# Stacked one-pass attention scores, earlier release of expert weight buffers, and two buffers instead of four in the third expert layer of a four-layer graph and mixture-of-experts kernel

## The chip, the cores and the metric

The kernel runs on one core of a Trainium2 chip. The metric is device time in microseconds (us) of the whole program; smaller is better. Unmarked times below are microseconds.

Engines are named as the profile names them: PE is TensorE, DVE is VectorE, ACT is ScalarE, POOL is GpSimd, SP is SyncE, which here only issues DMAs. PE has a clock with two levels, 1.2 and 2.4 GHz; "half clock" below means the lower.

## The reference, cut to what matters

1024 tokens (graph nodes) of 256 features pass four layers. Each layer adds a graph attention or graph convolution to x, then a mixture of experts with two experts per token:

```python
x = x + _L0_gnn_ref(_layernorm(x), neigh, edge_emb, adj, ...)
x = x + _L0_ffn_ref(_layernorm(x)[None], ...)[0]
# likewise layers 1, 2 and 3

# layer 0, attention scores (32 hidden features)
neib_att = jnp.tanh(neigh @ Wn1 + bn1) @ Wn2 + bn2
x_att    = jnp.tanh(x @ Wx1 + bx1) @ Wx2 + bx2
e_att    = jnp.tanh(edge_emb[adj] @ We + be)
ws = x_att @ neib_att.T + jnp.einsum('nkh,nh->nk', e_att, x_att)
ws = jax.nn.leaky_relu(ws, 0.01)
ws = jnp.where(adj > 0, ws, jnp.float32(-9000000000000000.0))
ws = jax.nn.softmax(ws, axis=1)

# layer 2, mixture of experts: 8 routed experts, hidden size 1024, and a shared one
shared = gelu(x @ W1s + b1s) @ W2s + b2s
rw = jax.nn.softmax(x @ Wr, axis=-1)
topw, topi = jax.lax.top_k(rw, K)          # K = 2
topw = topw / jnp.sum(topw, axis=-1, keepdims=True)
mask = jnp.sum(jax.nn.one_hot(topi, E) * topw[..., None], axis=-2)
h = gelu(jnp.einsum('bsd,edf->bsef', x, W1p) + b1p)
priv = jnp.einsum('bsef,efd->bsed', h, W2p) + b2p
return shared + jnp.einsum('bsed,bse->bsd', priv, mask)
```

Layer 0 has 16 experts of hidden size 512 with relu, layer 1 has 8 of 512 with gelu, layer 3 has 16 of 512 with a gated silu and no output bias. The adjacency is an integer matrix of zeros and ones, so the edge term takes one of two values per token.

## The kernel before, in words

All engines run programs of their own that meet by semaphores; the order on each engine is the order in which its code is written. Tokens stand in eight tiles of 128 partitions.

**Attention (L209 to L361).** It works in units of 128 query tokens against all 1024 neighbours (eight units in layer 0; more in layer 1, one per tile and head). For unit u: PE computes the scores into the PSUM tile S (`scores`, L516 to L520, layer 0 only; in layer 1 they are a sum of a row and a column and need no matmul). DVE adds the mask and takes the row maximum (`mask`, L241, into g). POOL works out two per-row biases in six tiny operations (L280 to L286). ACT makes the sloped copy (L297, into t2). DVE takes the larger of the two branches (`shift`, L249, into lm). PE transposes lm in eight pieces into the PSUM tile tp (`turn`, L336). ACT takes the exponential from tp (L306, into pT). PE multiplies by the values (`weigh`, L346). DVE divides (L523, L524). In the PE program a step runs turn(u-2), then scores(u+1), which waits until mask(u) has read S, then weigh(u-3). DVE runs mask(u), shift(u-2) and the ending of u-4. There is one S of two PSUM banks, and there are two tp of two banks each.

Ahead of it (the phase p0 of the function that holds L364 to L541) the two score operands g_xa and g_na, 32 partitions of 1024 fp32 values, come out of a matmul (L434) and a DVE operation that adds the bias (L493).

**Experts (L1194 to L1466).** The two choices of each token are sorted by expert into tiles of 128 rows; every expert has whole tiles of its own. Layer 2 has eight tiles for the shared expert ahead of them. The tiles run in rounds of UN = 4: lane b takes every fourth tile, and tile t = 4i + b uses buffer b of the weights w1, w2, b2, of the input rows xs, the output rows ys and the two index columns idx and to. The number of rounds is read at run time. A weight load is issued only when the expert of the tile differs from the one that its buffer holds. A round is never cut, so the tile count is a multiple of four.

For tile t:

- SP (L1262 to L1285) waits for y_ready of tile t-UN, that is for the last use of buffer b, then issues w1, w2 and b2.
- POOL (L1289 to L1315) runs load(t), which gathers 128 rows from DRAM into xs (L1308; a plain copy, L1302, for the shared tiles) once tile t-UN has been turned; then store(t-UN-1), which waits for y_ready of that tile and scatters ys to DRAM (L1293).
- PE runs turn(t) (L1333, transposes xs), rise(t-1) (L1345, first matmul, 32 or 16 pieces), fall(t-2) (L1358, second matmul in three passes of rounded parts).
- ACT runs w2_hi(t) (L1381, rounds w2), the activation of t (L1393; for silu L1386), h_hi(t) (L1397, rounds h).
- DVE runs copy(t) (L1408) and the next index column (L1413), split_w2(t-1) (L1425), split_h(t-1) (L1430), end(t-2) (L1438 and L1440: adds b2, writes ys, signals y_ready).

After the last tile the stored rows are read back and combined (L1125 to L1191), into the SBUF of the w1 buffers.

## Time and profile before

| | |
|---|---|
| median of 3 runs | 1261.8 us (1258.81 to 1266.55) |
| profiled execution | 1265.98 us |
| its span in the trace | 1264.0 us (1.98 us lie outside) |
| mean granted PE clock | 0.863 of full |
| PE busy over the span | 964.2 us (76%) |
| DVE, ACT, POOL busy | 740.7, 511.2, 452.2 us |

The stages that the change touches, as stretches of the trace in us from the span's start:

| stage | stretch | PE busy | PE clock |
|---|---|---|---|
| attention of layer 0 | 49 to 109 | 48.79 of 60 | 0.77 |
| experts of layer 0 | 152 to 246 | 83.98 of 94 | 0.98 |
| experts of layer 1 | 476 to 560 | 74.84 of 84 | 0.97 |
| experts of layer 2 | 697 to 905 | 207.00 of 208 | 0.99 |
| experts of layer 3 | 1092 to 1236 | 142.47 of 144 | 0.98 |

A row of the timeline gives start, duration, engine, line of the kernel, operation, tiles out<-in and shapes; a number before "x" is how many pieces stand in the row, and square brackets give the idle time of the engine just before it and what ended it. A tile name in the trace has its buffer number left out, so e_xs is any of the xs buffers of a layer. "DMA e_w<-w_in" is a weight load, "DMA e_b<-b_in" a load of b2.

### The profile page before, as it was taken

To read this page: it belongs to the slowest core of one execution; us is meant where nothing else is said; L and a number is where in the kernel's file an instruction comes from. 1 tells how busy PE (TensorE), PEld (TensorE's weight loads), DVE (VectorE), ACT (ScalarE), POOL (GpSimd) and SP (SyncE) were. 2 spreads that over 40 slices of the span, in tenths; PEclk is the share of its full clock that TensorE was granted. 3 is DMA by queue.
4 is the path that set the end of the run, shared out by engine and by line. 5 is a ranking of instruction groups with operands and counts; after the bars stand their busy time and mean duration, and the time that the engine had idled before them with its cause. 6 is when DMAs were issued, how large, how long until landed. Compare 5 with 4: busy or idle time off the path is not lost. (4 is left out here: it accounts for less than half of the span.)

```text
span 1264.0 us, 22113 instructions
## 1 busy us (share of the span) xinstructions
PE 964.2 (76%) x7102; PEld 875.1 (69%) x7102; DVE 740.7 (59%) x1712; ACT 511.2 (40%) x941; POOL 452.2 (36%) x572
## 2 busy tenths in 40 slices
PE   5786389808688738955973999999928995499993
PEld 1555288804677738854873899999914884499993
DVE  4435567664688655657434566666553674566664
ACT  2032067600366516642101777777603551243441
POOL 1031246410599514630000255555303440244431
PEclk9677599957799958987995899999958996699997
DMA  6001296520000015743112654653240001544764
GB/s 217 1 1 35 88 316 221 166 85 7 1 1 1 2 56 186 254 158 104 55 30 96 263 199 166 235 196 128 76 129 1 1 1 35 219 155 160 249 238 160
DMA packets 65605, 148.31 MB, mean 117 GB/s; under 512 B 10464, under 2 KB 42496, under 8 KB 59520
## 3 DMA queue, kind: packets, MB, share of 16 engines
q1 hardware_dynamic: 55552, 120.17, 27.7%
q0 software_dynamic: 9984, 27.28, 6.4%
q8 instruction: 37, 0.61, 0.2%
q14 instruction: 32, 0.26, 0.1%
HBM read 203.88 MB, written 18.87 MB: 176 GB/s over the span
## 5 line engine op out<-in xcount | busy, mean ns | idle before, releaser
L1345 PE MATMUL r_pH<-e_xsT,e_w 128*128 128x128 f32 x2624 | 319.4, 280 | 13.8 <-DMA e_w<-w_in 9.7
L1345 PEld LDWEIGHTS r_pH<-e_xsT,e_w 128*128 128x128 f32 x2624 | 308.1, 196 | 20.1 <-issue 12.9
L1293 POOL DMA_INDIRECT y_rows<-e_ys,e_to x104 | 179.3, 1724 | 264.3 <-DVE e_idx L1413 145.3
L1381 ACT ACTIVATE e_w_hi<-e_w 128x1024 fp32r<-128x1024 f32 (+1 forms) x104 | 136.4, 1312 | 128.8 <-DMA e_b<-b_in 95.0
L1425 DVE TENSOR_TENSOR e_w_lo<-e_w,e_w_hi 128x1024 fp32r<-128x1024 f32 (+1 forms) x104 | 161.0, 1548 | 40.7 <-ACT e_w_hi L1381 28.5
L1358 PE MATMUL r_pY<-e_w_hi,e_h_hi 128*128 128x256 f32 x544 | 163.0, 300 | 10.1 <-issue 8.2
L1430 DVE TENSOR_TENSOR e_h_lo<-xnT,e_h_hi 128x512 fp32r<-128x512 f32 (+1 forms) x104 | 89.1, 857 | 124.4 <-ACT e_h_hi L1397 118.3
L1358 PE MATMUL r_pY<-e_w_hi,e_h_lo 128*128 128x256 f32 x544 | 154.5, 284 | 0.0
L1358 PE MATMUL r_pY<-e_w_lo,e_h_hi 128*128 128x256 f32 x544 | 154.5, 284 | 0.0
L346 PE MATMUL g_o<-g_V,g_pT 128*128 128x65 f32 (+2 forms) x896 | 139.2, 310 | 15.3 <-ACT g_pT L306 15.2
L346 PEld LDWEIGHTS g_o<-g_V,g_pT 128*128 128x128 f32 x896 | 124.2, 195 | 31.4 <-issue 21.2
L1308 POOL DMA_INDIRECT e_xs<-xn_rows,e_idx x96 | 102.8, 1070 | 118.1 <-issue 112.2
L1393 ACT ACTIVATE xnT<-r_pH,e_w 128x128 f32<-128x128 f32 x432 | 119.0, 374 | 61.8 <-PE r_pH L1345 58.3
L297 ACT ACTIVATE g_t<-g_g,g_small 128x1024 f32<-128x1024 f32 x56 | 64.4, 1150 | 165.0 <-POOL g_small L286 165.0
L1358 PEld LDWEIGHTS r_pY<-e_w_hi,e_h_hi 128*128 128x128 f32 x544 | 104.7, 192 | 13.2 <-issue 12.7
L1358 PEld LDWEIGHTS r_pY<-e_w_lo,e_h_hi 128*128 128x128 f32 x544 | 105.0, 193 | 0.0
L1358 PEld LDWEIGHTS r_pY<-e_w_hi,e_h_lo 128*128 128x128 f32 x544 | 104.6, 192 | 0.0
L1397 ACT ACTIVATE e_h_hi<-xnT 128x512 fp32r<-128x512 f32 (+1 forms) x104 | 79.3, 762 | 24.1 <-DVE xnT L1420 19.2
L280 POOL TENSOR_TENSOR g_small<-g_small,g_s 128x1 f32<-128x1 f32 x56 | 28.9, 516 | 156.8 <-DVE g_small L241 156.7
L249 DVE SCALAR_TENSOR_TENSOR g_lm<-g_g,g_small,g_t 128x1024 f32<-128x1024 f32 x56 | 71.8, 1282 | 15.5 <-PE g_tp L336 9.5
L121 POOL TENSOR_SCALAR mean_var<-mean_var 128x8 f32<-128x8 f32 x9 | 2.5, 281 | 208.7 <-DVE mean_var L132 192.4
L336 PE MATMUL g_tp<-ident,g_lm 128*128 128x128 f32 x448 | 62.8, 287 | 16.3 <-DVE g_lm L249 15.6
(247 smaller groups left out, 1396.1 us busy)
## 6 DMA issues: line engine op xcount, KB each, us to landing
e_w<-w_in SPq DMA_DIRECT2D x60, 1024.0 KB
e_w<-w_in SPq DMA_DIRECT2D x72, 512.0 KB
e_w<-w_in SPq DMA_DIRECT2D x32, 1028.0 KB
e_w<-w_in SPq DMA_DIRECT2D x44, 514.0 KB
e_b<-b_in SPq DMA_DIRECT2D x76, 128.0 KB
e_w<-y_rows SPq DMA_DIRECT2D x24, 256.0 KB, 5.1
p_adj<-adj_in SPq DMA_DIRECT2D x8, 512.0 KB, 7.0
xn_rows<-xn SPq DMA_DIRECT2D x4, 1024.0 KB, 4.4
```

The lines of the kernel that those rows point to most:

```text
L249: nc.vector.scalar_tensor_tensor(out=lm[u % 2][:, :], in0=g[u % 4][:, :], scalar=b1[:, u:u + 1], in1=t2[u % 4][:, :], op0=ALU.add, op1=ALU ...
L297: nc.scalar.activation(t2[u % 4][:, :], g[u % 4][:, :], ACT.Identity, bias=b2[:, u:u + 1], scale=slope).then_inc(sloped, 1)
L346: ins = nc.tensor.matmul(o[u % 2][:, 0:width], pT[u % 2][:, c, :], values(u, c), start=(c == 0), stop=(c == NT - 1))
L1293: pool.indirect_dma_start(out=y_rows[:, :], in_=ys[b][:, :], in_offset=None, out_offset=bass.IndirectOffsetOnAxis(ap=to[b][:, :], axis=0))\
L1308: pool.indirect_dma_start(out=xs[b][:, :], out_offset=None, in_=xn_rows[:, :], in_offset=bass.IndirectOffsetOnAxis(ap=idx[b][:, :], axis=0))\
L1345: ins = nc.tensor.matmul(pH[b % 2][:, f, :], w1[b][:, at:at + P], xsT[b % 2][:, c, :], start=(c == 0), stop=(c == DC - 1))
L1358: ins = nc.tensor.matmul(pY[m][:, :], h[m][:, f, :], w[m][:, f * D:(f + 1) * D], start=(f == 0 and n == 0), stop=(f == FC - 1 and n == 2))
L1381: nc.scalar.activation(w2_hi[b % 2][:, :], w2[b][:, :], ACT.Copy).then_inc(w2_rounded, 1)
L1393: ins = nc.scalar.activation(hT[b % 2][:, f, :], pH[b % 2][:, f, :], ACT.Relu if kind == "relu" else ACT.Gelu, bias=b1)
L1397: nc.scalar.activation(h_hi[b % 2][:, :, :], hT[b % 2], ACT.Copy).then_inc(h_rounded, 1)
L1425: nc.vector.tensor_tensor(w2_lo[b % 2][:, :], w2[b][:, :], w2_hi[b % 2][:, :].bitcast(F32), ALU.subtract).then_inc(w2_split, 1)
L1430: nc.vector.tensor_tensor(h_lo[b % 2][:, :, :], hT[b % 2], h_hi[b % 2][:, :, :].bitcast(F32), ALU.subtract).then_inc(h_split, 1)
```

## The change

It has three parts.

**A, attention of layer 0.** The operands g_xa and g_na become 96 partitions of the fp32r type: a rounded copy and a remainder, stacked as (high, low, high) against (high, high, low), so that one pass of a 96-row product gives the three partial products. The weights of the matmul ahead are repeated two or three times (three DVE copies), ACT writes the rounded copy over 96 partitions (a new operation of 96x1024, twice), and DVE subtracts over 32 partitions where it added the bias before. Five small bias DMAs are added on SP behind the adjacency loads. S has two buffers and tp one (`deep = 1`). PE starts with scores(0) and scores(1), and then runs scores(u+2) ahead of turn(u-2).

**B, all expert layers.** SP issues w1 once the activation of tile t-UN is done (h_ready; for silu once the first matmul is done, h_summed), w2 once its split is done (w2_split), and b2 two tiles later with a semaphore of its own, b2_loaded. ACT's rounding of w2 no longer waits for b2; DVE's end does. The combine reads into the buffers of w1 and w2.

**C, experts of layer 2.** UN is 2 instead of 4 there: two buffers of everything, rounds of two tiles, four static rounds for the shared tiles. The per-tile tables that depend on UN exist for both values (four more tiny DVE operations at the start).

The core of the diff:

```diff
-UN = 4
+UN_NARROW, UN_WIDE = 4, 2
...
-            tp = [ph.ps(f"tp{n}", [P, NT, P]) for n in range(2)]
+            deep = 1 if scores else 2
+            tp = [ph.ps(f"tp{n}", [P, NT, P]) for n in range(deep)]
...
                     for hf in range(2):
-                        if u >= 2:
-                            pe.wait_ge(exped, 2 * (u - 2) + hf + 1)
+                        if u >= deep:
+                            pe.wait_ge(exped, 2 * (u - deep) + hf + 1)
...
                 if scores:
-                    scores(0).then_inc(scored, 1)
+                    for u in range(2):
+                        scores(u).then_inc(scored, 1)
                 for u in range(units + 3):
+                    if scores and u + 2 < units:
+                        pe.wait_ge(maxed, u + 1)
+                        scores(u + 2).then_inc(scored, 1)
                     if 2 <= u < units + 2:
                         turn(u - 2)
-                    if scores and u + 1 < units:
-                        pe.wait_ge(maxed, u + 1)
-                        scores(u + 1).then_inc(scored, 1)
...
-                xa = ph.sb("xa", [HID, N])
-                na = ph.sb("na", [HID, N])
+                xa = ph.sb("xa", [3 * HID, N], F32R)
+                na = ph.sb("na", [3 * HID, N], F32R)
...
+                        act.wait_ge(again_loaded, 16 * len(again))
+                        for n, (t, ps) in enumerate(((xa, psA), (na, psB))):
+                            act.wait_ge(mm, 3 + n)
+                            nc.scalar.activation(t[:, :].rearrange("p (a b) -> p a b", a=2), ps[0:3 * HID, :, :],
+                                                 ACT.Identity, bias=cols[:, 2 * n + 1:2 * n + 2]).then_inc(rounded, 1)
...
-                        for n, (t, ps) in enumerate(((xa, psA), (na, psB))):
-                            dve.wait_ge(mm, 3 + n)
-                            nc.vector.tensor_scalar(t[:, :].rearrange("p (a b) -> p a b", a=2), ps[0:HID, :, :],
-                                                    cols[:, 2 * n + 1:2 * n + 2], None, ALU.add).then_inc(copied, 1)
+                        for n, (t, lo, ps) in enumerate(((xa, X_LO, psA), (na, N_LO, psB))):
+                            dve.wait_ge(rounded, n + 1)
+                            halves = t[lo, :].rearrange("p (a b) -> p a b", a=2)
+                            nc.vector.scalar_tensor_tensor(out=halves, in0=ps[lo, :, :],
+                                                           scalar=cols[lo, 2 * n + 1:2 * n + 2],
+                                                           in1=halves.bitcast(F32), op0=ALU.add,
+                                                           op1=ALU.subtract).then_inc(copied, 1)
...
+            UN = un = UN_WIDE if shared else UN_NARROW
+            HEAD = max(2, first // UN)
...
                         if not early(i, b, UN):
-                            sp.wait_ge(y_ready, t - UN + 1)
+                            sp.wait_ge(h_summed if kind == "silu" else h_ready, t - UN + 1)
+                            sp.nop(nofuse=True)
                             held = sp.value_load(etab[0:1, bass.ds(t - UN, 1)], min_val=0, max_val=EN - 1)
                             other = {"cond": e != held}
                         sp.dma_start(w1[b][:, :], w1_v[bass.ds(e, 1), :, :].rearrange("a p c -> (a p) c"), **other)\
                             .then_inc(w1_loaded[b], 16)
+                        if not early(i, b, UN):
+                            sp.wait_ge(w2_split, t - UN + 1)
+                            sp.nop(nofuse=True)
                         sp.dma_start(w2[b][:, :], w2_v[bass.ds(e, 1), :, :].rearrange("a p c -> (a p) c"), **other)\
                             .then_inc(w2_loaded[b], 16)
-                        if b2_name:
-                            sp.dma_start(b2[b][:, :], A[b2_name][bass.ds(e, 1), :].to_broadcast([P, D]), **other)\
-                                .then_inc(w2_loaded[b], 16)
+                        if b2_name and not early(i, b, 2):
+                            bias(*before(i, b, 2))
...
-                        act.wait_ge(w2_loaded[b], W2_INC * (i + 1))
+                        act.wait_ge(w2_loaded[b], 16 * (i + 1))
...
                         if b2_name:
+                            dve.wait_ge(b2_loaded[b], 16 * (i + 1))
                             ins = nc.vector.tensor_tensor(ys[b][:, :], pY[b % 2][:, :], b2[b][:, :], ALU.add)
```

**Where it moves instructions: POOL, experts of layer 2.** This is the body of the run-time loop over the rounds of routed tiles, in the kernel before. L1308 is the gather into buffer n of xs, L1293 the store of the rows of a finished tile.

```order
L1308 DMA e2_xs0<-xn_rows,e2_idx0 128x256
L1291 ISA
L1293 DMA y_rows<-e2_ys3,e2_to3 6144x256
L1305 REGISTER_ALU
L1306 REGISTER_ALU
L1308 DMA e2_xs1<-xn_rows,e2_idx1 128x256
L1291 ISA
L1293 DMA y_rows<-e2_ys0,e2_to0 6144x256
```

After, the whole loop body is two tiles long (L1356 is the gather, L1341 the store).

```order
L1356 DMA e2_xs0<-xn_rows,e2_idx0 128x256
L1339 ISA
L1341 DMA y_rows<-e2_ys1,e2_to1 6144x256
L1354 REGISTER_ALU
L1356 DMA e2_xs1<-xn_rows,e2_idx1 128x256
L1339 ISA
L1341 DMA y_rows<-e2_ys0,e2_to0 6144x256
L1278 UNCONDITIONAL_BRANCH
```

The alternation of gather and store is the same. Before, the gather of tile t+1 stands behind the store of tile t-5 (buffer 3, when t has buffer 0); after, it stands behind the store of tile t-3, two tiles younger.

**PE, attention of layer 0, its first units.** Before (L518 scores, L336 transposes of turn, L346 weigh):

```order
L518 MATMUL g0_S<-g0_na,g0_xa 128x512 [waits g0_maxed]
L518 MATMUL g0_S<-g0_na,g0_xa 128x512
L336 MATMUL g0_tp0<-ident,g0_lm0 128x128 [waits g0_shifted]
L336 MATMUL g0_tp0<-ident,g0_lm0 128x128 x7
L518 MATMUL g0_S<-g0_na,g0_xa 128x512 [waits g0_maxed]
L518 MATMUL g0_S<-g0_na,g0_xa 128x512
L336 MATMUL g0_tp1<-ident,g0_lm1 128x128 [waits g0_shifted]
L336 MATMUL g0_tp1<-ident,g0_lm1 128x128 x7
```

After (L543 scores, L338 turn):

```order
L543 MATMUL g0_S0<-g0_na,g0_xa 128x512 [waits g0_maxed]
L543 MATMUL g0_S0<-g0_na,g0_xa 128x512
L338 MATMUL g0_tp0<-ident,g0_lm0 128x128 [waits g0_shifted]
L338 MATMUL g0_tp0<-ident,g0_lm0 128x128 x7
L543 MATMUL g0_S1<-g0_na,g0_xa 128x512 [waits g0_maxed]
L543 MATMUL g0_S1<-g0_na,g0_xa 128x512
L338 MATMUL g0_tp0<-ident,g0_lm1 128x128 [waits g0_exped,g0_shifted]
L338 MATMUL g0_tp0<-ident,g0_lm1 128x128 x3
```

In the piece of before, the scores ahead of turn(0) are those of unit 2 and stand directly behind mask(1); after, they are those of unit 4, and units 0 to 4 have been scored before turn(1). The second turn now also waits for an exponential, since there is one tp.

**SP, experts of layer 0, one step of the loop.** Before:

```order
L1269 ISA [waits e0_y_ready]
L1269 TENSOR_LOAD etab
L1269 ISA x2
L1271 REGISTER_ALU x2
L1271 ISA
L1271 DMA e0_w10<-w1_0_in 128x1028
L1273 ISA
L1273 DMA e0_w20<-w2_0_in 128x1024
L1276 ISA
L1276 DMA e0_b20<-b2_0_in 128x256
```

After:

```order
L1300 ISA [waits e0_h_ready]
L1300 TENSOR_LOAD etab
L1300 ISA x2
L1302 REGISTER_ALU x2
L1302 ISA
L1302 DMA e0_w10<-w1_0_in 128x1028
L1307 ISA [waits e0_w2_split]
L1307 DMA e0_w20<-w2_0_in 128x1024
```

Behind this piece the step goes on with a table read, a wait for y_ready and the DMA of b2 for the tile two before. The load of w1 now waits for the activation, that of w2 for the split, and that of b2 has moved behind them with a wait of its own.

## Rows read from the trace of the kernel before

**Rows 1.** Windows: the expert stages of layers 0, 1, 2, 3.

```profile
core 0: us, PE busy (x) PEld busy (x) DVE busy (x) ACT busy (x) POOL busy (x), PEclk, DMA share, GB/s
...
152.00:246.00 94.00, 83.98 (x674) 79.54 (x675) 60.02 (x135) 61.29 (x136) 51.15 (x42) 0.98 0.76 249
476.00:560.00 84.00, 74.84 (x600) 71.28 (x600) 53.65 (x120) 55.74 (x121) 44.12 (x36) 0.97 0.60 198
697.00:905.00 208.00, 207.00 (x1778) 206.24 (x1777) 129.23 (x179) 156.98 (x311) 103.81 (x57) 0.99 0.52 187
1092.00:1236.00 144.00, 142.47 (x1221) 141.23 (x1222) 87.97 (x185) 59.24 (x80) 61.34 (x49) 0.98 0.63 219
```

**Rows 2.** Timeline, attention of layer 0, one unit at half clock.

```profile
64.06 1.97 PE L336 MATMUL g_tp<-ident,g_lm 128*128 128x128 f32 x8 [2.52 <-DVE g_lm L249]
...
65.96 3.78 PE L518 MATMUL g_S<-g_na,g_xa 32*128 32x512 f32 x4
...
70.92 1.28 DVE L249 SCALAR_TENSOR_TENSOR g_lm<-g_g,g_small,g_t 128x1024 f32<-128x1024 f32 x1
...
72.26 0.93 PEld L336 LDWEIGHTS g_tp<-ident,g_lm 128*128 128x128 f32 x5 [4.10 <-DVE g_lm L249]
```

**Rows 3.** Timeline, attention of layer 0: turns 5, 6 and 7 at full clock.

```profile
92.60 1.09 PE L336 MATMUL g_tp<-ident,g_lm 128*128 128x128 f32 x8 [0.68 <-DVE g_lm L249]
...
98.26 1.09 PE L336 MATMUL g_tp<-ident,g_lm 128*128 128x128 f32 x8 [0.68 <-DVE g_lm L249]
...
103.99 1.04 PE L336 MATMUL g_tp<-ident,g_lm 128*128 128x128 f32 x8
```

**Rows 4.** Timeline, PE, attention of layer 1 (no scores): its turns 0 and 7.

```profile
329.89 1.97 PE L336 MATMUL g_tp<-ident,g_lm 128*128 128x128 f32 x8 [7.83 <-DVE g_lm L249]
...
354.46 1.04 PE L336 MATMUL g_tp<-ident,g_lm 128*128 128x128 f32 x8
```

**Rows 5.** Timeline, PE, layer 2: two successive one-pass matmuls of 256 columns.

```profile
651.22 0.28 PE L724 MATMUL g_pso<-g_high,g_mask 128*128 128x256 f32 x1
651.34 0.28 PE L724 MATMUL g_pso<-g_low,g_mask 128*128 128x256 f32 x1
```

**Rows 6.** Timeline, preparation of layer 0: ACT over 1024 columns, as the added one.

```profile
27.73 1.10 ACT L470 ACTIVATE p_tn<-p_psB,p_cols 32x1024 f32<-32x1024 f32 x1 [2.27 <-PE p_psB L427]
```

**Rows 7.** Waits in the window 152:246 (experts of layer 0): us, times, longest.

```profile
PE r_pH L1345 <- DMA e_w<-w_in: 5.8, 7, 2.0
```

**Rows 8.** Waits in the window 476:560 (experts of layer 1).

```profile
PE r_pH L1345 <- DMA e_w<-w_in: 2.8, 3, 1.6
```

**Rows 9.** Timeline, PE, experts of layer 0: the activation was late.

```profile
200.45 2.05 PE L1345 MATMUL r_pH<-e_xsT,e_w 128*128 128x128 f32 x16 [1.20 <-ACT xnT L1393]
```

**Rows 10.** Timeline, experts of layer 2, steady state: one tile.

```profile
784.88 0.38 PE L1333 MATMUL r_pT<-ident,e_xs 128*128 128x128 f32 x2
...
791.55 0.38 PE L1333 MATMUL r_pT<-ident,e_xs 128*128 128x128 f32 x2
...
793.37 0.42 DVE L1440 TENSOR_TENSOR e_ys<-r_pY,e_b 128x256 f32<-128x256 f32 x1
...
794.10 2.28 DVE L1425 TENSOR_TENSOR e_w_lo<-e_w,e_w_hi 128x2048 fp32r<-128x2048 f32 x1
794.56 2.67 POOL L1293 DMA_INDIRECT y_rows<-e_ys,e_to  x1 [2.72 <-DVE e_idx L1413]
...
797.53 0.97 POOL L1308 DMA_INDIRECT e_xs<-xn_rows,e_idx  x1 [0.30 <-issue]
```

**Rows 11.** Source L1333 in the window 690:905: transposes of layer 2, two a tile.

```profile
L1333 PE MATMUL r_pT<-ident,e_xs x64: 271/273/475, 696.7 to 898.3; 128*128 128x128 f32 x64
```

**Rows 12.** Timeline, POOL: a store in the experts of layer 0.

```profile
183.13 0.99 POOL L1293 DMA_INDIRECT y_rows<-e_ys,e_to  x1 [4.03 <-DVE e_idx L1413]
```

**Rows 13.** DMA view of 744.15:744.50 and 797.48:797.83: gathers, us to landing.

```profile
e_xs<-xn_rows,e_idx POOLq DMA_INDIRECT x1, 6.8
...
e_xs<-xn_rows,e_idx POOLq DMA_INDIRECT x1, 2.8
```

**Rows 14.** Timeline, POOL, experts of layer 2: the first store.

```profile
716.00 3.00 POOL L1293 DMA_INDIRECT y_rows<-e_ys,e_to  x1 [16.99 <-DVE e_ys L1440]
```

126 lines of the change are left out of this document (79 added, 47 removed).

## The prediction

> **What bounds the kernel now.** I read the page first for how full each engine is, then the windows by stage, because the three parts of the change touch stages with different limits, and then the timeline and the waits inside each stage. In the expert stages PE is the bound: in layer 2 it is busy 207.00 of 208 us, in layer 3 142.47 of 144; in layers 0 and 1 it stands idle 10.0 and 9.2 us [rows 1]. So in layers 2 and 3 there is nothing to win except PE work itself, and in layers 0 and 1 at most those gaps. In the attention of layer 0 it is a loop across engines that bounds. At half clock one unit takes 72.26 - 64.06 = 8.20 us, in which the scores alone are 3.78 [rows 2]: scores(u+1) waits for mask(u), mask for scores, and the transposes stand in the same PE queue behind a late shift. At full clock the unit takes 98.26 - 92.60 = 5.66 us, with PE still waiting 0.68 for the shift [rows 3]. The attention of layer 1 runs the same loop without scores; its turns 0 and 7 start at 329.89 and 354.46, so 24.57 us for seven units, a half-clock start included [rows 4].
>
> **Part A, attention of layer 0.** Scores become a one-pass product. Two one-pass matmuls of 256 columns start 0.12 us apart at full clock [rows 5], so 512 columns take 0.24 and a unit's two records 0.48. With two S buffers and the scores two units ahead, the scores leave the cross-engine loop. What is left is the loop of layer 1 with 0.48 us of PE added per unit: 24.57 + 7 x 0.48 = 27.9 us from turn 0 to turn 7. Before it is 103.99 - 64.06 = 39.9 [rows 2, 3]. That gives 12.0. The way to turn 0 held three scores in series with three masks; two of them, at 3.78 each [rows 2], leave it, 7.6 in all, of which I give back 1.0, since the POOL and ACT work of unit 0 then is what the first shift waits for: 6.6. Attention: -18.6. The single tp lets turn(u+1) start only after the exponential of u; weigh(u-1) stands between them on PE and is longer, so I cost it at nothing. If that cover were missing, it would cost one half of an exponential, about 0.6 a unit, 4 in all.
>
> In the preparation ACT gets two operations over 1024 columns like the one of 1.10 us [rows 6]. They take the place of the DVE operation ahead of the subtraction, and the second overlaps the first subtraction, so one of them and its handover stand on the path: +1.3 (bounds 1.1 and 2.5). The repeats of the weights and the five small DMAs stand beside the projections and the adjacency loads; I cost them at nothing, and with the cover gone they would be under 1. Part A: -17.3.
>
> **Part B, release of the weight buffers.** The release moves forward by more than one tile. Waits of PE for weights are 5.8 us in layer 0, in seven places, the longest 2.0 [rows 7], and 2.8 in layer 1, in three places [rows 8]. One more gap of 1.20 in layer 0 is a late activation [rows 9], which stands behind the rounding of w2 on ACT, and that waited for the b2 load that came last. Seven us in layer 0 is thus the most; some loads also compete for bandwidth (249 GB/s on the mean of this stage, [rows 1]) and an earlier issue does not make them shorter. I take 5 of 7 in layer 0, 3 in layer 1 and 1 of the 1.5 idle in layer 3 [rows 1]: -9, with bounds 0 and -14. The added waits on SP (w2_split, y_ready of an older tile) are for things that happened a tile before, so nothing queues behind them for long.
>
> **Part C, two buffers in layer 2.** First the gain. The stage turns 64/2 = 32 tiles [rows 11]. The routing of the reference's inputs gives the eight experts 950, 2, 8, 2, 1015, 50, 8 and 13 rows, hence 8+1+1+1+8+1+1+1 = 22 tiles, with the 8 shared ones 30. In rounds of four they are 32, in rounds of two 30. One tile takes 791.55 - 784.88 = 6.67 us of full PE [rows 10], so two tiles are -13.3.
>
> Then the price. POOL's order is gather(t), store(t-3), gather(t+1). Call T(s) the start of turn(s). The output rows of tile s-2 are complete at 793.37 + 0.42 = 793.79, that is T(s) + 8.91 with T(s) = 784.88; the store starts at T(s) + 9.68 and takes 2.67; the gather behind it starts 0.30 later [rows 10]. With four buffers that gather is for a tile four turns after s and has two tiles of slack. With two buffers it is the gather for tile s+2, so T(s+2) cannot be before T(s) + 9.68 + 2.67 + 0.30 + L = T(s) + 12.65 + L, L the time from the gather's issue to its landing. A gather takes 2.8 with no weights moving and 6.8 in the midst of a weight load [rows 13]. At L = 2.8 two tiles take 15.45 instead of 13.33: PE, full until now, waits 2.12 us in each pair, since turn(s+2) stands ahead of rise(s+1) and fall(s) in its queue.
>
> Weights change at tiles 8 and 9 and at 24 to 29, four pairs. There I take L = 4.3, nearer to the quiet value, because the loads are issued some 6 us before the gather: 16.95, +3.6 a pair. From tiles 4 and 5 on there are twelve pairs: 8 x 2.12 + 4 x 3.6 = 31.4. The loop is entered late as well: the first store runs from 716.00 to 719.00 [rows 14], and gather 4 now stands behind it; with 0.30 and 2.8, T(4) is 722.1, against 784.88 - 10 x 6.67 = 718.2: +3.9. Part C: -13.3 + 31.4 + 3.9 = +22.
>
> Bounds. If every store took the 0.99 us of a store of layer 0 [rows 12], the pair would be 13.77, the twelve pairs +5.3, the entry +1.9, and part C -6. With L = 6.8 in the four loading pairs it is 8 x 2.12 + 4 x 6.1 + 3.9 - 13.3 = +32; in all twelve, which nothing in the quiet tiles speaks for, +64.
>
> Which store applies is told by the trace: it lasts from 794.56 to 797.23, across the DVE operation L1425 (794.10 to 796.38), and a store of layer 0 that stands free takes 0.99 [rows 10, 12]. The extra 1.7 us is about what is left of the DVE operation when the store starts. In the slower loop both still hang on the same event, so I keep 2.67. The Trainium skill, "SBUF — State Buffer", section "Who interferes with whom", bears on this from both sides. A DVE instruction with two SBUF inputs, as L1425 is, contends with a GpSimd instruction that reads SBUF, and the one that comes second is blocked for the whole instruction: by that rule, the trace agrees. The same section infers that a tensor_tensor takes only the read side and leaves descriptor generation alone: by that the store would cost 0.99 and part C be -6; the 2.67 of this trace is against it.
>
> **The sum.** -17.3 - 9 + 22 = -4.3 on the profiled 1265.98 gives 1261.7. The profiled execution is 4.2 above the median of the runs; scaled by 1261.8/1265.98 the forecast is 1257.
>
> **The rivals.**
>
> B: the gather is not late in layer 2. It needs the store to be free of DVE and the gather short, so that the pair stays near 13.3; or weight loads in this loop that move DVE's work away from the store. Then part C is -13 to -6, and the sum -40 to -32: about 1222 to 1230 on the median. For it speaks only that free stores are 0.99 [rows 12]; against it the 2.67 in the steady tile and that even then 13.77 is over 13.33. Chance 0.1.
>
> C, on the slower side: weights and gathers collide more than I take. With two buffers a new expert's 2 MB are asked for only one tile ahead, and the gathers of neighbouring tiles fall into them, also the weight itself can be late for rise. If L is 6.8 in the loading pairs and the loads are late by 2 us in each of the eight loading tiles, part C is +32 + 16 = +48 and the time 1265.98 - 26 + 48 = 1288, or 1284 on the median. It decides from about +39 on. Chance 0.13.
>
> D: part A gives half. PE stays at half clock for most of the attention: the unit then costs twice its PE work, 2 x 3.6 = 7.2, against 8.20 [rows 2], and only the way to turn 0 and the last units gain, about 9 instead of 18.6. The time is 1267. For it speaks that PE has run at half clock until the middle of this stage (8.20 then 5.66); against it that in layer 1 the same loop lost only one or two us to half clock [rows 4] and that PE has fewer gaps after the change. Chance 0.12.
>
> E: part B does nothing, since the loads are bound by bandwidth: 1266. It is a shift inside the forecast's range more than a case of its own. Chance 0.05.
>
> **How the numbers follow.** Forecast 0.6, B 0.1, C 0.13, D 0.12, E 0.05. The likeliest is 1257, its own range 1245 to 1270. For 8 in 10 the range reaches down into the space between it and B and up to the lower part of C: 1238 to 1279. About 1% is what a measurement can tell, so below 1249.2 counts as faster and above 1274.4 as slower. Faster: B, and a quarter of the forecast with part C nearer +14: 0.28. Slower: C, and the tails of D and E: 0.16. Between them 0.56.
>
> **What the profile after would show.** Part A right: turn 7 of layer 0 about 18 us earlier, the time between turns near 3.6 to 4. Part B right: PE's waits for weights in layers 0 and 1 near zero. Part C right: 60 transposes instead of 64; PE's clear waits for "DMA e_xs<-xn_rows,e_idx" at every second turn, of 2 us, where there are none before; turn starts 15.4 us apart over two tiles in the quiet stretch; the gather on POOL right behind a store of 2.7. Part C wrong: turns 6.67 apart, or waits for e_w. The prediction fails by most if the store takes 1 us in layer 2 or the gathers take over 5.

## The result and the profile after

The changed kernel takes 1294.86 us (median of 4 runs, 1290.83 to 1296.89) against 1260.8 of the kernel before on the same chip: a ratio of 1.025, 95% interval 1.0214 to 1.0286. It is slower by 2.5%, on the other side of the forecast of 1257 and outside its range of 1238 to 1279.

The two traces, laid side by side at the same events (us from the span's start; a stage of experts goes from the first transposes of its tiles to the read-back of the stored rows):

| | before | after | difference |
|---|---|---|---|
| scores(0) starts | 49.95 | 51.43 | +1.5 |
| from there to turn 7 of the attention, layer 0 | 54.0 | 29.3 | -24.7 |
| experts of layer 0 | 105.0 | 113.1 | +8.2 |
| experts of layer 1 | 86.5 | 89.9 | +3.4 |
| experts of layer 2 | 224.9 | 269.5 | +44.6 |
| experts of layer 3 | 157.7 | 155.5 | -2.2 |
| span | 1264.0 | 1291.9 | +27.9 |

The attention of layer 0 gave more than forecast, and of the four expert stages two came out with the other sign (layers 0 and 1) and one at twice its size (layer 2). Four turns of the attention after, timeline of PE, which answer to [rows 2, 3]:

```profile
57.57 1.97 PE L338 MATMUL g_tp<-ident,g_lm 128*128 128x128 f32 x8 [0.58 <-DVE g_lm L251]
...
65.23 1.04 PE L338 MATMUL g_tp<-ident,g_lm 128*128 128x128 f32 x8
...
68.37 1.04 PE L338 MATMUL g_tp<-ident,g_lm 128*128 128x128 f32 x8
...
80.74 1.04 PE L338 MATMUL g_tp<-ident,g_lm 128*128 128x128 f32 x8
```

Turn 0 comes 6.1 us after scores(0), against 14.1 before, and a unit with scores at full clock takes 3.14 (65.23 to 68.37) where it took 5.66. PE is at half clock only for the first two units.

The four expert stages after, windows by stage, which answer to [rows 1]:

```profile
core 0: us, PE busy (x) PEld busy (x) DVE busy (x) ACT busy (x) POOL busy (x), PEclk, DMA share, GB/s
129.00:242.00 113.00, 94.11 (x720) 90.28 (x720) 64.56 (x144) 66.27 (x144) 57.23 (x45) 0.92 0.63 212
459.00:549.00 90.00, 76.20 (x600) 73.89 (x600) 53.51 (x120) 55.72 (x121) 48.50 (x37) 0.94 0.58 189
683.00:952.00 269.00, 228.65 (x1740) 223.89 (x1738) 127.56 (x174) 152.60 (x301) 88.96 (x58) 0.89 0.30 104
1122.00:1278.00 156.00, 150.03 (x1288) 149.28 (x1288) 92.58 (x196) 62.08 (x85) 67.24 (x52) 0.98 0.60 207
```

In layer 2 PE runs fewer matmuls than before (30 tiles), yet is busy longer than those need, at a mean granted clock of 0.89 of full where it was 0.99, and 40 us idle. (A timeline row splits a group of matmuls where a window of the view begins, so a rise can stand in one row or in two.) One pair of quiet tiles there, timeline, which answers to [rows 10]:

```profile
790.24 0.43 PE L1381 MATMUL r_pT<-ident,e_xs 128*128 128x128 f32 x2 [2.02 <-DMA e_xs<-xn_rows,e_idx]
790.58 5.44 PE L1393 MATMUL r_pH<-e_xsT,e_w 128*128 128x128 f32 x32
...
791.07 0.97 POOL L1341 DMA_INDIRECT y_rows<-e_ys,e_to  x1 [2.71 <-PE r_pT L1381]
...
792.35 1.98 POOL L1356 DMA_INDIRECT e_xs<-xn_rows,e_idx  x1 [0.30 <-issue]
...
798.72 0.38 PE L1381 MATMUL r_pT<-ident,e_xs 128*128 128x128 f32 x2
798.94 3.74 PE L1393 MATMUL r_pH<-e_xsT,e_w 128*128 128x128 f32 x32
...
800.55 0.42 DVE L1489 TENSOR_TENSOR e_ys<-r_pY,e_b 128x256 f32<-128x256 f32 x1
...
801.74 2.67 POOL L1341 DMA_INDIRECT y_rows<-e_ys,e_to  x1 [7.41 <-DVE e_ys L1489]
...
804.71 0.97 POOL L1356 DMA_INDIRECT e_xs<-xn_rows,e_idx  x1 [0.30 <-issue]
...
807.60 0.43 PE L1381 MATMUL r_pT<-ident,e_xs 128*128 128x128 f32 x2 [2.06 <-DMA e_xs<-xn_rows,e_idx]
```

The chain of the prediction is there link by link: output rows done at 800.97, store from 801.74 for 2.67, gather at 804.71, landed 2.89 later, PE waiting 2.06. What the prediction did not have is in the second row: the rise behind the wait takes 5.44 instead of 3.74. The mean granted clock from 790.58 to 796.00 is 0.69, and from 798.94 to 802.40, in the next rise, 1.00. PE works part of the first at half clock, so the output rows come 10.73 after the turn and not 8.91, and the pair takes 807.60 - 790.24 = 17.36 instead of 15.45.

In layer 0 PE's waits for weights, which were 5.8 us [rows 7], more than doubled (waits view of the window 129:242, changed kernel):

```profile
PE r_pH L1393 <- DMA e_w<-w_in: 12.2, 7, 3.4
```

The same view shows a wait that DVE does not have in the kernel before, where it is ACT that waits for b2. DVE's end of a tile now waits for it, since it is issued two tiles later:

```profile
DVE e_ys L1489 <- DMA e_b<-b_in: 15.2, 13, 3.1
```

And SP has become slow. Its DMA issues in layer 0, timeline of SP, changed kernel (L1302 w1, L1307 w2, L1324 b2):

```profile
166.08 0.34 SPq L1302 DMA_DIRECT2D e_w<-w_in  x1
166.77 0.33 SPq L1307 DMA_DIRECT2D e_w<-w_in  x1
168.67 0.33 SPq L1324 DMA_DIRECT2D e_b<-b_in  x1
170.71 0.33 SPq L1302 DMA_DIRECT2D e_w<-w_in  x1
```

A step of SP takes 4.63 us here, which is also the median of the stage, while a full tile of PE takes 3.43 there. In the kernel before the median step was 3.75. After w2 it goes on for 1.90 us before b2 is issued: two reads of the expert table stand between them.

### The profile page after: what moved, and what is told of

Its sections match the earlier page's. It is cut to its first block and busy times, and to the rows that moved or that the text cites. A ratio compares the mean times of both kernels' runs of the same rounds, so it can differ in the third digit from the quotient of the medians.

```text
span 1291.9 us, 22826 instructions
## 1 busy us (share of the span) xinstructions
PE 959.2 (74%) x6970; PEld 883.3 (68%) x6970; DVE 732.0 (57%) x1707; ACT 504.7 (39%) x923; POOL 439.1 (34%) x568
## 3 DMA queue, kind: packets, MB, share of 16 engines
q1 hardware_dynamic: 53632, 109.01, 24.7%
## 5 line engine op out<-in xcount | busy, mean ns | idle before, releaser
L1393 PE MATMUL r_pH<-e_xsT,e_w 128*128 128x128 f32 x2560 | 338.2, 294 | 21.2 <-DMA e_w<-w_in 17.4
L1393 PEld LDWEIGHTS r_pH<-e_xsT,e_w 128*128 128x128 f32 x2560 | 327.0, 210 | 27.0 <-issue 17.6
L1341 POOL DMA_INDIRECT y_rows<-e_ys,e_to x102 | 163.9, 1607 | 330.6 <-DVE e_ys L1489 195.6
L1429 ACT ACTIVATE e_w_hi<-e_w 128x1024 fp32r<-128x1024 f32 (+1 forms) x102 | 132.4, 1298 | 117.5 <-DMA e_w<-w_in 116.5
L1441 ACT ACTIVATE xnT<-r_pH,e_w 128x128 f32<-128x128 f32 x416 | 115.1, 376 | 128.9 <-PE r_pH L1393 128.9
L1473 DVE TENSOR_TENSOR e_w_lo<-e_w,e_w_hi 128x1024 fp32r<-128x1024 f32 (+1 forms) x102 | 156.0, 1530 | 14.9 <-ACT e_w_hi L1429 14.2
L1406 PE MATMUL r_pY<-e_w_lo,e_h_hi 128*128 128x256 f32 x528 | 150.9, 286 | 0.0
L1406 PE MATMUL r_pY<-e_w_hi,e_h_lo 128*128 128x256 f32 x528 | 150.6, 285 | 0.0
L1356 POOL DMA_INDIRECT e_xs<-xn_rows,e_idx x94 | 105.2, 1119 | 116.7 <-issue 111.9
L1381 PE MATMUL r_pT<-ident,e_xs 128*128 128x128 f32 x204 | 43.1, 298 | 68.3 <-DMA e_xs<-xn_rows,e_idx 55.9
L1381 PEld LDWEIGHTS r_pT<-ident,e_xs 128*128 128x128 f32 x204 | 25.2, 148 | 72.9 <-issue 33.7
```

The lines of the kernel that those rows point to most:

```text
L1341: pool.indirect_dma_start(out=y_rows[:, :], in_=ys[b][:, :], in_offset=None, out_offset=bass.IndirectOffsetOnAxis(ap=to[b][:, :], axis=0))\
L1356: pool.indirect_dma_start(out=xs[b][:, :], out_offset=None, in_=xn_rows[:, :], in_offset=bass.IndirectOffsetOnAxis(ap=idx[b][:, :], axis=0))\
L1381: ins = nc.tensor.transpose(pT[b % 2][:, c, :], xs[b][:, c * P:(c + 1) * P], ident[:, :])
L1393: ins = nc.tensor.matmul(pH[b % 2][:, f, :], w1[b][:, at:at + P], xsT[b % 2][:, c, :], start=(c == 0), stop=(c == DC - 1))
L1406: ins = nc.tensor.matmul(pY[m][:, :], h[m][:, f, :], w[m][:, f * D:(f + 1) * D], start=(f == 0 and n == 0), stop=(f == FC - 1 and n == 2))
L1429: nc.scalar.activation(w2_hi[b % 2][:, :], w2[b][:, :], ACT.Copy).then_inc(w2_rounded, 1)
```

## The experiments

The theory after these readings has three parts. First, in layer 2 the gather stands behind a store that is too young, and the wait that this gives PE lowers its clock, so that each pair pays twice. Second, in layers 0 and 1 SP's own instructions have become the bound, since part B doubled its table reads. Third, part A is sound. The rivals: the new order of the weight loads costs, two buffers are too few as such, or earlier loads collide in the DMA engines.

The runs were taken in four groups. The kernel before ran beside each of them, and its median was 1260.8, 1263.0, 1262.9 and 1264.7 us. A difference between kernels of two groups is uncertain by these few us, and stages are compared within the traces.

**Four buffers in layer 2 again** (e1_four): part C undone.

```diff
-UN_NARROW, UN_WIDE = 4, 2
+UN_NARROW, UN_WIDE = 4, 4
```

> The changed kernel with four buffers and rounds of four in layer 2, parts A and B kept. In the two traces layer 2 (first turn to the read-back of the rows) went from 224.9 to 269.5 us, +44.6. Theory 'part C costs it all': the time falls by 44 to 48 us, to about 1247 to 1251, PE is full again in layer 2. Rival 'the new release order of the weight loads costs in layer 2 too': less than 35 us come back and waits for weights are seen in layer 2.

Measured: 1250.7 us, 44.1 under the changed kernel's 1294.9; layer 2 takes 225.0 us. Against the kernel before the ratio is 0.9881 (0.9847 to 0.9915). The whole loss of layer 2 is part C's, and parts A and B together are worth 12 us, although A alone gives 24 (below). In this trace layer 0 takes 113.4 us and layer 1 93.0, so part B costs there without part C too.

**The store one tile later** (e2_store_later): two buffers stay; POOL stores tile t-4 behind gather t.

```diff
+            LAG = 4 if UN == 2 else UN + 1
...
-                        if not early(i, b, UN + 1):
-                            store(*before(i, b, UN + 1), y_stored[(b - 1) % UN])
+                        if not early(i, b, LAG):
+                            store(*before(i, b, LAG), y_stored[(b - LAG) % UN])
...
-                    store(last - 1, UN - 1, y_stored[UN - 1])
+                    for b in range(2 * UN - LAG, UN):
+                        store(last - 1, b, y_stored[b])
```

> The changed kernel, but in layer 2 POOL stores tile t-4 behind gather t, not tile t-3; two buffers kept. Theory 'the gather stands behind a young store, its wait of 2.0 us at every second turn lowers the clock for the rise behind it': gathers are issued before they are needed, the waits of 2.0 us for e_xs and the rises of 5.4 us go, quiet tiles are 6.7 us apart, layer 2 gives back 44.6 and the two tiles, in all 45 to 58 us: 1234 to 1247. Rival 'two buffers are too few for anything: weights or output rows are late': at most half of that comes back, and waits for e_w or for the stored rows take the place of those for e_xs. Second rival: only the pairs in which weights are loaded stay long, then about 15 us less come back.

Measured: 1239.7 us, 55.2 under the changed kernel; layer 2 takes 215.9 us, 53.6 less than after and 9.0 less than before. The turns of its quiet stretch, timeline of PE, and the store and gather beside them, timeline of POOL:

```profile
792.32 0.38 PE L1383 MATMUL r_pT<-ident,e_xs 128*128 128x128 f32 x2
798.99 0.38 PE L1383 MATMUL r_pT<-ident,e_xs 128*128 128x128 f32 x2
805.66 0.38 PE L1383 MATMUL r_pT<-ident,e_xs 128*128 128x128 f32 x2
```

```profile
788.66 2.67 POOL L1342 DMA_INDIRECT y_rows<-e_ys,e_to  x1 [2.72 <-DVE e_ys L1491]
791.64 0.97 POOL L1357 DMA_INDIRECT e_xs<-xn_rows,e_idx  x1 [0.30 <-issue]
```

Turns are 6.67 apart, without a wait. The store still takes 2.67 and still stands ahead of a gather; only it is one tile older. So two buffers are enough for the weights and the rows in the quiet stretch, and what cost 54 us is the place of one instruction in POOL's order. (At the last tiles, which load new weights, two rises do wait for them, 1.71 and 1.16 us.)

**PE kept busy through the wait** (e4_filler): 14 transposes of the identity ahead of the turn of every even tile from tile 4 on.

```diff
                         if not early(i, b, 2):
                             pe.wait_ge(xsT_ready, t - 1)
+                        if UN == 2 and b == 0 and not early(i, b, 3):
+                            for _ in range(14):
+                                nc.tensor.transpose(pT[b][:, 0, :], ident[:, :], ident[:, :])
                         pe.wait_ge(xs_loaded[b], 16 * (i + 1))
```

> The changed kernel with 14 extra transposes of the identity on PE ahead of the waiting turn of each even tile from 4 on in layer 2, about 1.8 us of PE work in what is otherwise a wait of 2.0 us. Their result is overwritten. Theory 'the wait lowers the clock and the rise behind it pays 1.7 us': the clock stays up, rises take 3.74 instead of 5.4, quiet pairs take about 15.5 instead of 17.3, and the kernel gets 15 to 23 us faster although PE does more. Rival 'the rise is long for another reason': rises stay at 5.4 and the time stays or rises by up to 3 us.

Measured: 1279.5 us, 15.4 under the changed kernel; layer 2 takes 252.8 us, 16.7 less, and its mean granted clock is 0.97. Timeline of PE over one pair:

```profile
783.77 1.69 PE L1381 MATMUL r_pT<-ident 128*128 128x128 f32 x14
...
785.84 0.44 PE L1384 MATMUL r_pT<-ident,e_xs 128*128 128x128 f32 x2 [0.37 <-DMA e_xs<-xn_rows,e_idx]
...
786.16 3.81 PE L1396 MATMUL r_pH<-e_xsT,e_w 128*128 128x128 f32 x32
...
801.48 0.44 PE L1384 MATMUL r_pT<-ident,e_xs 128*128 128x128 f32 x2 [0.46 <-DMA e_xs<-xn_rows,e_idx]
```

PE does more and the kernel is faster: the rise is back at 3.81, and the pair takes 801.48 - 785.84 = 15.64, close to the 15.45 of the prediction. The long rise was the clock, and the idle stretch of PE ahead of it was its cause. The clock's share of part C is thus about 17 us.

**SP without its second pair of table reads** (e3_lean_sp): b2 of tile t is issued in the step of t.

```diff
-                        if b2_name and not early(i, b, 2):
-                            bias(*before(i, b, 2))
+                        if b2_name:
+                            if not early(i, b, UN):
+                                sp.wait_ge(y_ready, t - UN + 1)
+                                sp.nop(nofuse=True)
+                            sp.dma_start(b2[b][:, :], A[b2_name][bass.ds(e, 1), :].to_broadcast([P, D]), **other)\
+                                .then_inc(b2_loaded[b], 16)
```

> The changed kernel, but SP issues b2 of tile t in the step of tile t with the registers it has, so that two reads of the expert table a step go; w1 and w2 are still released early. In the trace of the changed kernel SP's steps in layer 0 are 4.1 to 5.0 us apart, a full PE tile takes 3.43. Theory 'SP's own instructions bound layers 0 and 1': steps come down to PE's pace, waits of PE for weights in layer 0 (13 us) and layer 1 (7 us) fall below those of the kernel before (5.8 and 2.8), total 10 to 20 us faster than the changed kernel. Rival 'earlier loads collide with gathers and each other, bandwidth is the bound': no change, within 4 us.

Measured: 1274.1 us, 20.7 under the changed kernel, with ten executions from 1264.2 to 1280.4. The profiled one is among the shortest, 1264.7 us, so its stages add up to more than the 20.7; why the executions differ by 16 us is open. In its trace layer 0 takes 96.0 us (113.1 in the changed kernel, 105.0 before) and layer 1 81.2 (89.9 and 86.5). SP's timeline in layer 0, and PE's wait for weights there (window 120:240):

```profile
172.01 0.34 SPq L1302 DMA_DIRECT2D e_w<-w_in  x1
172.70 0.34 SPq L1307 DMA_DIRECT2D e_w<-w_in  x1
173.37 0.33 SPq L1313 DMA_DIRECT2D e_b<-b_in  x1
175.51 0.33 SPq L1302 DMA_DIRECT2D e_w<-w_in  x1
```

```profile
PE r_pH L1383 <- DMA e_w<-w_in: 0.2, 1, 0.2
```

A step is 3.50 us instead of 4.63, b2 follows w2 after 0.67 instead of 1.90, and 12.2 us of waits shrink to 0.2. w1 and w2 are released as early as in the changed kernel, so collisions of the early loads are not the cause. The edit does two things at once, though: it takes out two reads, and it issues b2 two tiles earlier, which also ends DVE's 15.2 us of waits for b2. The next run tells how much the reads do alone. Two reads cost 1.90 - 0.67 = 1.23 us, 0.6 each. The Trainium skill, "DMA: Bandwidth & Descriptors", section "Latency and other measured facts", gives about 600 ns as the floor of a tensor_load: by that, the trace agrees.

**The other way round: the kernel before with two idle reads** (e5_before_reads).

```diff
+                        if b2_name and not early(i, b, UN):
+                            sp.value_load(etab[0:1, bass.ds(t, 1)], min_val=0, max_val=EN - 1)
+                            sp.value_load(etab[0:1, bass.ds(t - UN, 1)], min_val=0, max_val=EN - 1)
                         if b2_name:
```

> The kernel before, with two more reads of the expert table on SP in every step from tile 4 on in layers 0, 1 and 2; their values are not used, nothing else moves. Theory 'SP's steps bound layers 0 and 1': layer 0 (first turn to read-back, 105.0 us before) gets 8 to 16 us longer, layer 1 (86.5) 3 to 10, layer 2, where a tile takes 6.7 us, nothing; the time rises by 11 to 26 us. Rival 'the changed order of the loads is what costs': no change within 3 us.

Measured: 1272.1 us, 9.2 over the kernel before (1.0062, 1.0037 to 1.0087). Layer 0 takes 111.0 us (+6.0), layer 1 89.3 (+2.8), layer 2 224.8 (unchanged). The total and both increments are under the low ends of what was expected, the sign and the place are as expected. PE's waits for weights in layer 0 (window 152:264):

```profile
PE r_pH L1348 <- DMA e_w<-w_in: 12.4, 11, 1.8
```

They were 5.8 in the kernel before, and the sum is that of the changed kernel, 12.2, without anything of its load order. Here they are eleven short waits, there seven longer ones, up to 3.4 us. So the reads alone lengthen layer 0 by 6.0 us, where the whole change lengthened it by 8.2, and layer 1 by 2.8, where it was 3.4, but the picture is not the same. PE runs the same 720 matmuls of layer 0 in all four traces (windows over the whole stage):

| layer 0 | stage | PE busy | PE idle | PE clock |
|---|---|---|---|---|
| before | 105.0 | 90.05 | 14.95 | 0.98 |
| changed kernel | 113.1 | 94.11 | 18.99 | 0.92 |
| before with two idle reads | 111.0 | 90.41 | 20.59 | 0.98 |
| changed kernel, lean SP | 96.0 | 87.75 | 8.25 | 0.96 |

Half of the 8.2 us of the changed kernel is PE at a lower clock and not PE idle. No run separates the late b2 from the reads in the changed kernel.

**Part A alone** (e7_a_only): the changed kernel with four buffers, one release at y_ready for w1, w2 and b2, and ACT waiting for b2.

```diff
-                            sp.wait_ge(h_summed if kind == "silu" else h_ready, t - UN + 1)
+                            sp.wait_ge(y_ready, t - UN + 1)
...
-                        if not early(i, b, UN):
-                            sp.wait_ge(w2_split, t - UN + 1)
-                            sp.nop(nofuse=True)
...
-                        act.wait_ge(w2_loaded[b], 16 * (i + 1))
+                        act.wait_ge(w2_loaded[b], (32 if b2_name else 16) * (i + 1))
```

> Part A alone: four buffers in layer 2, w1, w2 and b2 released together at y_ready and ACT waiting for b2 as in the kernel before; the read-back still uses the w1 and w2 buffers. Theory 'part A gives the 23 us that the trace of the changed kernel shows at the first expert turn, and nothing of it is given back': 22 to 27 us under the kernel before, 1236 to 1241; layer 0 at 105 us, layer 1 at 86.5. Rival 'earlier arrival in layer 0 is lost in later stages': 1246 or more.

Measured: 1238.6 us, ratio 0.9791 (0.976 to 0.9822). Layer 0 takes 105.8 us, layer 1 85.6, layer 2 225.2. Part A gives 24 us against the kernel before of its own group, and none is lost later.

**Part A with four-pass scores** (e8_four_pass): the same, but the product runs over the 32 rows of the rounded parts in fp32.

```diff
-                        ins = nc.tensor.matmul(S[u % 2][:, hf, :], xa[:, u * P:(u + 1) * P],
-                                               na[:, hf * 512:(hf + 1) * 512], start=True, stop=True)
+                        ins = nc.tensor.matmul(S[u % 2][:, hf, :], xa[0:HID, u * P:(u + 1) * P].bitcast(F32),
+                                               na[0:HID, hf * 512:(hf + 1) * 512].bitcast(F32), start=True, stop=True)
```

> Part A alone, but the scores are taken as an fp32 product of the rounded parts over 32 rows, four passes as before, with the new order and the two S buffers; the two small partial products are left out. It tells the pass count from the order. Theory 'the order with two S buffers gives most': the attention (scores 0 to turn 7, 54.0 us before, 29.3 after) is at 36 to 42 us, 1.5 us of PE more a unit at full clock and more at half. Rival 'the passes give most': 46 us or more.

Measured, one execution: 1252.3 us; the attention, scores(0) to turn 7, takes 95.45 - 51.93 = 43.5 us, between the two expectations. It is 54.0 before and 79.73 - 51.59 = 28.1 with part A alone. So of the 25.9 us the order with two S buffers gives 10.5 and the single pass, on top of it, 15.4. Neither expectation was right, the pass count is the larger part.

**Both repairs everywhere** (e6_a_lean_c_later): the edits of e2_store_later and e3_lean_sp together.

> The changed kernel with both repairs: b2 issued without own table reads, and in layer 2 the store one tile later. If the two causes are independent the gains add: 1239.7 less 20.8 (or less 25.8 by the stages of the trace), so 1213 to 1220, faster than the kernel before by 3.4 to 4%. Rival 'they overlap': 1228 or more, with waits for weights back in layer 2.

Measured: 1235.0 us (0.9788, 0.9741 to 0.9836). The gains do not add; the rival holds. Layers 0 and 1 are at 96.7 and 81.4, but layer 2 is at 235.2 instead of 215.9. PE's waits there (window 650:895):

```profile
PE r_pH L1385 <- DMA e_w<-w_in: 16.6, 5, 5.9
```

With b2 in the step of its own tile, SP waits for y_ready of tile t-2 before it comes to w1 of tile t+1. With four buffers that is an event of the past, with two it is the newest one. SP's timeline has w2 at 861.90 and the b2 behind it only at 865.29, then w1 of the next tile at 867.34. In layer 2 the b2 issue two tiles later, which is what costs the reads, is needed; the next run tests it.

**Each repair where it belongs** (e10_best): the late store and the changed kernel's SP in layer 2, the lean SP in layers 0 and 1.

```diff
-                        if b2_name and not early(i, b, 2):
-                            bias(*before(i, b, 2))
+                        if b2_name and UN == UN_WIDE:
+                            if not early(i, b, 2):
+                                bias(*before(i, b, 2))
+                        elif b2_name:
```

> The changed kernel with the store one tile later in layer 2, and b2 issued without own table reads in layers 0 and 1 only; layer 2 keeps b2 two tiles behind. With both repairs everywhere, layer 2 took 235.2 us instead of 215.9, with 16.6 us of waits for weights on PE: there b2's wait for y_ready stood ahead of the next tile's w1. Theory: layer 0 about 96.5, layer 1 about 81.3, layer 2 about 216 us, total 1235.0 - 19.3 = 1216, at the least 1209 and at most 1222. Rival 'the shorter layer 2 depends on the late arrival of something else': 1228 or more.

Measured: 1217.1 us (1215.8 to 1219.2), ratio 0.9625 (0.9595 to 0.9654), as expected. Layers 0 to 3 take 97.7, 81.2, 217.9 and 153.9 us.

**The same with four buffers in layer 2** (e9_a_lean_four).

> The same without part C: four buffers in layer 2, b2 without own table reads in all layers. It shows what part B gives once SP keeps up: against part A alone (1238.6) layer 0 goes from 105.8 to 96.5, layer 1 from 85.6 to 81.3, layer 3 by 1 to 2: 1222 to 1226. And what two buffers give with a gather in time: 8 to 10 us between this and the kernel above. Rival 'two buffers give nothing': the two are within 3 us.

Measured: 1225.4 us, ratio 0.9694 (0.9661 to 0.9727); layers 0 to 3 at 97.3, 80.6, 224.7 and 155.4. Part B is worth 12 to 13 us over part A alone once SP keeps up, and two buffers with a gather in time are worth 8 more, of the 13.3 that two tiles take.

**Parts A and C without B** (e11_a_and_c).

> Parts A and C without part B: two buffers in layer 2, weights released at y_ready, as in the kernel before. The store stays at tile t-3. Theory: quiet pairs as in the changed kernel, 17.3 us, since the release of weights has no part in them; in the eight tiles with new weights the loads, asked for about 9 us after the turn of the tile before, are 4 to 7 us late, so layer 2 takes 269.5 + 32 to 56 = 300 to 325 us. Rival 'the early release is what lengthens quiet pairs': pairs of 15.5 and layer 2 under 270.

Measured, one execution: 1399.6 us, layer 2 385.5. Both expectations fail, mine by 60 us. No gather is waited for in the quiet stretch; every rise waits for "weights", also where none are loaded. Timelines of SP and of PE (L1302 w1, L1365 turn, L1377 rise):

```profile
890.03 0.07 SPq L1302 DMA_DIRECT2D e_w<-w_in  x1
```

```profile
886.76 0.38 PE L1365 MATMUL r_pT<-ident,e_xs 128*128 128x128 f32 x2
...
890.33 3.81 PE L1377 MATMUL r_pH<-e_xsT,e_w 128*128 128x128 f32 x32 [3.19 <-DMA e_w<-w_in]
...
896.85 0.38 PE L1365 MATMUL r_pT<-ident,e_xs 128*128 128x128 f32 x2
```

The issue of 0.07 is a skipped load. Its semaphore counts only when SP comes to it, and SP waits for y_ready of the tile that holds the buffer. With two buffers that event is one of the loop itself: the output rows of a tile are complete (here at 889.00) 8.7 us after the rise of the tile behind it has started, SP needs 1.0 to pass, and only then may the next rise start, at 890.33. So even a tile that loads nothing takes 896.85 - 886.76 = 10.09. I had priced only the tiles that load. Among the orders that ran, two buffers pay only with part B; without it no run has the later store.

## Why the prediction was wrong, point by point

**Part A, sized too small.** Forecast -18.6 in the attention and +1.3 in the preparation; measured -24.7 and +1.5. The failing term is 24.57 + 7 x 0.48: 27.9 us from turn 0 to turn 7 were forecast and 80.74 - 57.57 = 23.2 came, and turn 0 itself came 1.4 earlier after scores(0) than forecast. The sum adds seven groups of scores, but with the scores two units ahead only three stand between turn 0 and turn 7 (at 59.20, 64.68 and 67.81), so four groups, 1.9 us, were added that are not there. The 24.57 of layer 1 was also too long as a model: its third turn, at 337.06, still takes 1.82 us, while here the third is back at 1.04, and 1.4 us less than the 24.57 came even with the scores. Why the other 2.8 us did not come is in part that, and otherwise not taken apart. The single tp, costed at nothing, shows once, as a wait of 0.99 us for the exponential at 78.05. Rival D, half clock for most of the stage, did not come.

**Part B, wrong in sign.** Forecast -9; measured +8.2 in layer 0, +3.4 in layer 1, -2.2 in layer 3, +9.4 in all. The step that failed is the sentence "The added waits on SP (w2_split, y_ready of an older tile) are for things that happened a tile before, so nothing queues behind them for long". The waits are not what the runs point at; the instructions between them, two table reads of 0.6 us in every step, were not priced, and e5_before_reads shows that they alone give +6.0 and +2.8. What the later b2 does on DVE was put at nothing as well, and its share is not known. The order rows of SP, before and after, showed more table reads per step, and SP's timeline of the kernel before shows how close a step was to a tile: from w1 to w1 3.69 us in layer 0, where a full tile takes 3.43.

```profile
203.51 0.34 SPq L1271 DMA_DIRECT2D e_w<-w_in  x1
204.16 0.35 SPq L1273 DMA_DIRECT2D e_w<-w_in  x1
204.91 0.33 SPq L1276 DMA_DIRECT2D e_b<-b_in  x1
207.20 0.33 SPq L1271 DMA_DIRECT2D e_w<-w_in  x1
```

(Timeline of SP, layer 0, kernel before.) SP had next to no slack there, which I had not read, since the page of the profile counts no busy time for it. The gain that I forecast does exist, -9 in layer 0 and -5 in layer 1, as e3_lean_sp shows, if the reads go.

**Part C, right in mechanism, half in size.** Forecast +22; measured +44.6. The gather behind the store of tile t-3 came out, and within 0.1 us each so did the 0.77 from the output rows to the store, the 2.67, the 0.30 and the landing of 2.8 in the quiet pairs; so did the saving of two tiles. What failed is the constant 8.91 between a turn and the output rows: it was taken from a stretch in which PE was never idle, and the very wait that I computed makes the rise behind it 1.7 us longer. With it the 9.68 from a turn to the store became 11.50 (790.24 to 801.74). From turn 4 to turn 28, twelve pairs, the changed kernel takes 919.95 - 705.77 = 214.2 us where 8 x 15.45 + 4 x 16.95 = 191.4 were forecast: 22.8 over. Added up over the pairs of the trace, 19.4 of that is a store that starts more than 9.68 after its turn, and 3.3 is the way from the store to the next turn. There the gathers of the four pairs that I priced at 4.3 landed after 4.0, 4.6, 4.9 and 6.3 us. e4_filler gives back 17 by taking away nothing but the idleness of PE. That 22.8 is so near to the miss of the whole term is partly luck: the entry cost 1.7 and not 3.9, and the last turn came 2.0 later than forecast, and the two cancel. Rival C was on the right side of zero and named a minor cause: gathers do land late beside weight loads, which is the 3.3 us, but PE has no waits for weights in layer 2 after the change, and the gathers of the quiet stretch land in 2.7 to 2.9. The choice of 2.67 for the store was right; that it speaks against the inference which the prediction quotes was not, as the last section shows.

**The sum.** Forecast -4.3; measured +27.9 on the span. Of the miss of 32, part C is 23 and part B 18. Part A takes back 6 and the stretches between the stages 3, which is luck and not the forecast. The chance of 0.16 for slower was too small: I gave no rival to SP, and none to the clock.

## What to carry to other kernels

When buffers are halved, go through each in-order queue and ask which event each instruction now stands behind: here the same alternation of gather and store with the store one tile too young cost 54 us, and moving one store by one tile turned the change from +2.5% to -2.2%. Price the issuing engine as you do the others: two table reads of 0.6 us each on SP were free at 6.7 us a tile and cost 6 us of layer 0 at 3.4 us a tile; taking them out of the changed kernel, with b2 issued earlier by the same edit, gave 17 there. And when a forecast puts a regular wait of 2 us on PE in a stretch where it was always busy, price a variant in which the matmuls behind it run in part at the lower clock.

## What the runs showed of the hardware

**A wait of 2 us on PE can cost nearly as much again.** In the changed kernel the rise behind a wait of 1.88 to 2.06 us took 5.29 to 5.44 us instead of 3.74, six times out of six, at a mean granted clock of 0.68 to 0.70 over the rise. Behind waits of 1.27 and 1.34 us in the same stage it took 3.74, at a granted clock of 1.00 (timeline of PE, changed kernel):

```profile
720.59 0.44 PE L1381 MATMUL r_pT<-ident,e_xs 128*128 128x128 f32 x2 [1.27 <-DMA e_xs<-xn_rows]
...
720.87 3.74 PE L1393 MATMUL r_pH<-e_xsT,e_w 128*128 128x128 f32 x32
```

It is not the length of one wait alone: in e11_a_and_c a rise behind 3.19 us of waiting ran in 3.81, at a granted clock of 1.00. What decides was not found.

**Who starts first matters between POOL and DVE.** In the pair shown above the store at 791.07 takes 0.97, since it starts ahead of the two-input subtraction on DVE, and the gather behind it, beside that subtraction, takes 1.98; at 801.74, within the next subtraction, the store takes 2.67 and the gather after it 0.97. The Trainium skill, "SBUF — State Buffer", section "Who interferes with whom", says that the order of issue decides who blocks: by that rule, the trace agrees as far as POOL is concerned. That DVE is the one to wait when POOL is first does not show: the subtraction takes 2.28 us in both cases. The same section infers that a tensor_tensor leaves descriptor generation alone, and the 2.67 is not against that: an indirect DMA also reads an index column (e_to, e_idx) in SBUF. A plain copy that POOL issues has none, and one that started within such a two-input subtraction took 0.56, as much as the others, at 0.55 (timeline, kernel before):

```profile
718.91 1.23 DVE L1430 TENSOR_TENSOR e_h_lo<-xnT,e_h_hi 128x1024 fp32r<-128x1024 f32 x1 [0.86 <-ACT e_h_hi L1397]
719.00 0.56 POOL L1302 DMA_DIRECT2D e_xs<-xn_rows  x1
```

The same copy took 0.56 in e9_a_lean_four, where 2.17 us of the subtraction were still to come.

**A skipped load is not free of its place.** Its semaphore counts when the issuing engine comes to it, so a tile that loads nothing still waits for the release of its buffer (10.09 us a tile in e11_a_and_c).

Why two tiles less are worth 8 to 9 us and not 13.3 even with the gather in time can be read off e2_store_later: from the first turn to the last it is 10.5 us shorter than the kernel before, since single turns come late, the latest by 1.9 us behind a wait for new weights, and from the last turn to the read-back it takes 24.85 us instead of 23.44.

What stays open: how much the late b2 costs in layers 0 and 1, when a wait of PE lowers its clock, and what the entry of the loop costs, with stores ahead of the copies of the shared tiles, which was not tried apart.
